# Two grouped attentions: outputs turned by VectorE in blocks of 32 instead of by TensorE, half-groups of 128 tokens by four heads

## The chip, the cores and the metric

The kernel runs on one core of one Trainium2 chip. The time is the device time of one execution in microseconds (us). Three executions of the kernel before took 3545.53, 3547.29 and 3551.32 us; the median, 3547.29 us, is the number to beat. Engines are named as in the profile: PE is TensorE's matmul, PEld its weight load, DVE is VectorE, ACT is ScalarE, POOL is GpSimd, SP is the engine that issues most transfers.

## The reference

Eight layers run one after another on x, 4 batches of 256 tokens by 256 numbers, with a context of 1601 tokens. The change touches the second and the sixth, which are grouped attentions with 16 query heads, 4 key heads and heads of 128 numbers. The sixth, cut to what matters:

```
q = rms_norm((x @ Wq).reshape(B, 256, 16, 128), q_norm_w)
k = rms_norm((ctx @ Wk).reshape(B, S_enc, 4, 128), k_norm_w)
v = (ctx @ Wv).reshape(B, S_enc, 4, 128)
scores = einsum('bhqd,bhkd->bhqk', q, repeat(k, 4)) / 128 ** 0.5
out = einsum('bhqk,bkhd->bqhd', softmax(scores), repeat(v, 4))
x = x + out.reshape(B, 256, 2048) @ Wo
```

The second layer does the same, but its keys and values come from the context and the 256 tokens of x together, and queries and keys are rotated by their positions (`rope`).

## The kernel before

`grouped_attention` is called once for each of the two layers (stage a1 with `rope` True, stage a3 with False). Work is cut into 16 groups, one for each batch and key head. A group holds 4 query heads by 256 tokens, which are 8 blocks of 128 columns, and is done in two units of 512 columns. A unit walks over all key tiles of 128 tokens, 15 in a1 and 13 in a3, and one such tile is a turn.

In each turn PE computes scores for a key tile (`scores`, three products of 512 columns, L1176 to L1178), then does what tasks stand in that turn's entry of `GROUP_TURNS`, then adds probabilities times values of the tile 21 turns back in a1, 19 in a3 (`values`, L1188). ACT moves scores from PSUM into a ring (`keep`, L1309) and takes the exponential of an older tile (`exp`, L1324). DVE keeps the running maximum (`highest`, L1572), subtracts a maximum from some tiles (`shift`, L1589) and POOL subtracts it from the others (`shift`, L1436). Each engine has its own instruction list in a fixed order, and semaphores tie them: `scores` of a turn waits for `highest` of two turns before, because there are two score banks.

In the entries of `GROUP_TURNS`, KV, Q, KX, QX, OX, Y and others are tasks of the next group or the last one. Most use one of three PSUM banks in turn. The tasks that the change touches are these:

- `outputs` on DVE runs when the last value product of a unit is done, in turns 6 and 21 of a group in a1 and in turns 6 and 19 in a3. It divides by the row sums (L1597, L1598) and writes `o_rows`, tokens down and head dimension across. PE's next unit of value products waits for it (`o_done`).
- OX turns `o_rows` for the output product: four PE transposes (L1122) into a bank, ACT's copy into the high half `ot[0]` (L1296), and DVE's subtraction into the low half `ot[1]` (L1489, in the helper `low`). It is in turns 12 and 23 of a1, 8 and 21 of a3.
- Y is the output product, 12 matmuls of 256 columns for each block of 128 tokens (L1133). It waits for OX of both halves.
- QX turns queries for the next group; in the kernel before one half is two heads by 256 tokens.
- `end_turn`, `end_high`, `end_low` and `end_products` do the same for the last group, behind the last turns.

## Time and profile before

| | |
|---|---|
| median of 3 runs | 3547.29 us |
| profiled execution, whole | 3551.81 us |
| profiled execution, span from the first to the last instruction | 3550.1 us |
| first scores of a1 to its last | about 527 to 1621 us of the span |
| first scores of a3 to its last | about 2421 to 3386 us of the span |
| PE busy | 3300.8 us, 93% |
| DVE busy | 2283.9 us, 64% |
| ACT busy | 2250.7 us, 63% |
| POOL busy | 1545.9 us, 44% |

The profile lists single instructions with start, duration, what they write and read, and the idle time of their engine before them with what ended it. Matmuls overlap one another, so what one of them costs is read from the start of the first to the start of what follows, not from its own duration. One value product shows as two matmul records, since the trace has two passes for it, so `values` of a turn are 8 records; a transpose shows as one.

### The profile page before, as it was taken

Reading aid. Unit: us, or ns where it says so; the run is one execution under the profiler, and the core shown is the slowest. Engines: PE = TensorE matmul, PEld = TensorE weight load, DVE = VectorE, ACT = ScalarE, POOL = GpSimd, SP = SyncE. Lnnn points to the kernel's source line nnn. Section 1 sums busy time; section 2 is a strip of 40 time slices with the busy share of each in tenths; the row PEclk is TensorE's granted clock in tenths of the full one; section 3 lists DMA queues with packets and bytes.
Section 4 is the critical chain, followed back from the end, with each engine's and each line's share of the span. In section 5 each row is a group of like instructions: output and inputs, shape, how many; then the busy total and the mean of one; then the engine's idle time right before and its main releaser. Section 6 shows DMA issues by size and latency. Waiting matters only on the chain. (4 is left out here: it accounts for less than half of the span.)

```text
span 3550.1 us, 64164 instructions
## 1 busy us (share of the span) xinstructions
PE 3300.8 (93%) x23332; PEld 2862.7 (81%) x23332; DVE 2283.9 (64%) x4549; ACT 2250.7 (63%) x5204; POOL 1545.9 (44%) x1568
## 2 busy tenths in 40 slices
PE   6858968999999999998899999897999999999999
PEld 5658967999989989997666665586999989999888
DVE  8976756776676676666777777435555555555544
ACT  3326746777777777774566676416777777777743
POOL 0012137767676667663121120203555555555534
PEclk8879979999999999999899999899999999999999
DMA  5206522211120120102101100213211121110011
GB/s 192 93 24 230 210 107 70 86 62 37 43 79 31 37 91 31 37 25 80 44 1 38 38 1 1 77 39 131 76 67 60 43 74 43 69 59 31 30 40 39
DMA packets 74457, 227.83 MB, mean 64 GB/s; under 512 B 7780, under 2 KB 29472, under 8 KB 69152
## 3 DMA queue, kind: packets, MB, share of 16 engines
q1 hardware_dynamic: 67538, 184.04, 14.6%
q0 software_dynamic: 3696, 37.68, 2.8%
q8 instruction: 188, 3.08, 0.4%
q10 hardware_dynamic: 2910, 2.01, 0.2%
q14 instruction: 125, 1.02, 0.1%
HBM read 178.60 MB, written 45.11 MB: 63 GB/s over the span
## 5 line engine op out<-in xcount | busy, mean ns | idle before, releaser
L1188 PE MATMUL ps<-a_v_rows,a_ring 128*128 128x129 f32 (+1 forms) x7168 | 937.2, 276 | 8.0 <-DVE a_o_rows L1598 6.4
L1572 DVE SCALAR_TENSOR_TENSOR a_peak<-ps,a_k_rstd,a_peak 128x512 f32<-128x512 f32 (+1 forms) x768 | 575.9, 750 | 569.5 <-ACT a_ring L1309 559.8
L1309 ACT ACTIVATE a_ring<-ps,a_k_rstd 128x512 f32<-128x512 f32 (+1 forms) x896 | 616.6, 689 | 476.2 <-PE ps L1178 433.3
L1188 PEld LDWEIGHTS ps<-a_v_rows,a_ring 128*128 128x128 f32 (+1 forms) x7168 | 877.5, 192 | 23.6 <-ACT a_ring L1324 7.1
L1436 POOL TENSOR_TENSOR a_ring<-a_ring,a_negb 128x512 f32<-128x512 f32 (+1 forms) x506 | 642.4, 1292 | 236.3 <-ACT a_negb L1318 228.4
L1324 ACT ACTIVATE a_ring<-a_ring 128x512 f32<-128x512 f32 (+1 forms) x896 | 563.6, 632 | 14.5 <-DVE a_ring L1589 9.4
L1176 PE MATMUL ps<-a_qt,a_kt 128*128 128x512 f32 (+1 forms) x896 | 424.6, 474 | 18.6 <-DVE a_peak L1572 14.3
L1076 PEld LDWEIGHTS ps<-a_wr,a_ct 128*128 128x128 f32 (+1 forms) x2496 | 353.0, 189 | 48.1 <-issue 13.6
L1076 PE MATMUL ps<-a_wr,a_ct 128*128 128x256 f32 (+1 forms) x2496 | 373.6, 287 | 13.5 <-DMA a_ct<-ctx_lo 13.3
L1178 PE MATMUL ps<-a_qt,a_kt 128*128 128x512 f32 (+1 forms) x896 | 355.4, 397 | 0.0
L1177 PE MATMUL ps<-a_qt,a_kt 128*128 128x512 f32 (+1 forms) x896 | 354.2, 395 | 0.0
L3431 ACT ACTIVATE a_probs<-ps 128x1024 f32<-128x1024 f32 x224 | 229.6, 1025 | 134.8 <-PE ps L3285 134.0
L1589 DVE TENSOR_TENSOR a_ring<-a_ring,ps 128x512 f32<-128x512 f32 x390 | 263.0, 677 | 2.8 <-ACT a_negb L1318 2.8
L3623 DVE TENSOR_REDUCE a_parts<-ps 128x1 f32<-128x448 f32 x384 | 222.2, 619 | 57.8 <-PE ps L3247 52.4
L1178 PEld LDWEIGHTS ps<-a_qt,a_kt 128*128 128x128 f32 (+1 forms) x896 | 166.1, 185 | 42.6
L1176 PEld LDWEIGHTS ps<-a_qt,a_kt 128*128 128x128 f32 (+1 forms) x896 | 169.3, 189 | 28.7 <-DVE a_peak L1572 20.8
L1177 PEld LDWEIGHTS ps<-a_qt,a_kt 128*128 128x128 f32 (+1 forms) x896 | 169.4, 189 | 1.6
L3285 PE MATMUL ps<-a_qt,a_kt 128*128 128x512 f32 x448 | 163.8, 447 | 2.5 <-ACT a_qt L3418 2.3
L1371 POOL TENSOR_SCALAR a_k_sq<-a_k_sq 128x4 f32<-128x4 f32 (+2 forms) x128 | 29.0, 226 | 311.0 <-ACT a_v_rows L1272 306.6
L1520 DVE TENSOR_TENSOR a_k_rows<-ps,a_kw 128x128 f32<-128x128 f32 (+1 forms) x448 | 126.6, 283 | 56.6 <-ACT a_v_rows L1272 56.4
L3247 PE MATMUL ps<-a_kt,a_qt 128*128 128x448 f32 (+1 forms) x512 | 154.9, 370 | 4.7 <-ACT a_kt L3399 1.1
L1268 ACT ACTIVATE a_square<-ps 128x128 f32<-128x128 f32 (+1 forms) x448 | 124.7, 278 | 33.0 <-PE ps L1076 26.4
(469 smaller groups left out, 6012.9 us busy)
## 6 DMA issues: line engine op xcount, KB each, us to landing
a_wr<-a_w SPq DMA_DIRECT2D x96, 512.0 KB, 4.3
a_w<-a_wr SPq DMA_DIRECT2D x32, 512.0 KB, 3.9
a_wr<-a_w SPq DMA_DIRECT2D x48, 256.0 KB, 3.7
a_ct<-ctx_hi SPq DMA_DIRECT2D x8, 1090.0 KB, 5.8
a_ct<-ctx_lo SPq DMA_DIRECT2D x8, 1090.0 KB, 8.8
f_we<-in_f_experts SPq DMA_DIRECT2D x8, 1088.0 KB, 9.1
ctx_hi<-a_ct SPq DMA_DIRECT2D x4, 1602.0 KB, 5.4
ctx_lo<-a_ct SPq DMA_DIRECT2D x4, 1602.0 KB, 9.4
```

The lines of the kernel that those rows point to most:

```text
L1076: ins = pe.matmul(out[0:r, 0:2 * HD], src, wr[0][v][:, c * 2 * HD:(c + 1) * 2 * HD], start=(n == 0), stop=(n == 3 * DC - 1))
L1176: pe.matmul(out, kt[0][:, at:at + r], qt[0][:, cols], start=True, stop=False)
L1177: pe.matmul(out, kt[0][:, at:at + r], qt[1][:, cols], start=False, stop=False)
L1178: pe.matmul(out, kt[1][:, at:at + r], qt[0][:, cols], start=False, stop=True).then_inc(st_ready, 1)
L1188: ins = pe.matmul(m.ps[:, 6 + i // 2, (i % 2) * 256:(i % 2) * 256 + VW], slot(n)[0:r, i * P:(i + 1) * P], v_rows[u // NG % 2][0:r, t, :], ...
L1309: act.activation(slot(n)[0:r, :], m.ps[0:r, SCORE_BANKS[n % 2], :], ACT.Copy, scale=k_rstd[0:r, g % 2, t:t + 1]).then_inc(kept, 1)
L1324: act.activation(slot(n)[0:r, :], slot(n)[0:r, :], ACT.Exp).then_inc(exp_done, 1)
L1436: pool.tensor_tensor(slot(n)[0:r, :], slot(n)[0:r, :], negb[0:r, u % 2, :], ALU.add)\
L1572: dve.scalar_tensor_tensor(out=peak[0:r, :], in0=m.ps[0:r, SCORE_BANKS[n % 2], :], scalar=k_rstd[0:r, u // NG % 2, t:t + 1], in1=(slot(n - ...
L1589: dve.tensor_tensor(slot(n)[0:r, :], slot(n)[0:r, :], m.ps[0:r, MAX_BANK, :], ALU.add)\
L3431: act.activation(flat2(probs[n % 3][:, :, :]), flat2(m.ps[:, first:first + 2, :]), ACT.Exp)\
L3623: dve.tensor_reduce(to, slot(("R", h, j))[:, 0:n], AX.X, ALU.max, negate=True).then_inc(neg_done, 1)
```

## The change

Three things change together.

First, a unit holds four heads of 128 tokens instead of two heads of 256 tokens. QX transposes the same eight blocks, but ACT and DVE write them so that a block of 128 columns is 4 heads by 32 tokens. Such a block becomes the rows of the unit's output.

Second, OX no longer exists on PE. `outputs` ends with one DVE instruction that transposes every 32 by 32 square of the half of `o_rows` in place. After it, rows are 4 heads by 32 dimensions and columns are tokens, which is a valid left operand of the output product, once the rows of `wo` are laid out in the same order (in `lay_gqa`, before the launch). ACT and DVE then make the high and low halves from `o_rows` in SBUF instead of from a PSUM bank, in the same places of their lists.

Third, Y of a block of 128 tokens needs only its own unit, so it waits for one low half (`o_lo`) and not for both.

```
@@ scores, queries, outputs: views @@
+            def queries_of(k, i):
+                return qt[i][:, k * 512:(k + 1) * 512].rearrange("p (i h t) -> p h i t", h=REP, t=32)
+            def turned_outputs(k, i):
+                return ot[i][:, k * 512:(k + 1) * 512].rearrange("p (b i t) -> p i b t", b=P // 32, t=32)
+            def output_blocks(k):
+                return o_rows[:, k * JG:(k + 1) * JG, :].rearrange("p i (b t) -> p i b t", t=32)
@@ PE @@
                     def QX(g, k):
-                        for i in range(4):
-                            j = 4 * k + i
-                            ins = pe.transpose(out[:, i * P:(i + 1) * P], q_rows[:, j % QT, j // QT, :], m.ident[:, :])
-                    def OX(g, k):
-                        out = begin(("OX", g, k))
-                        pe.wait_ge(o_done, NG * (g - 1) + k + 1)
-                        for i in range(4):
-                            ins = pe.transpose(out[:, i * P:(i + 1) * P], o_rows[:, 4 * k + i, :], m.ident[:, :])
-                        ins.then_inc(item_ready, 1)
+                        for h in range(REP):
+                            ins = pe.transpose(out[:, h * P:(h + 1) * P], q_rows[:, k, h, :], m.ident[:, :])
                     def Y(g, q):
-                        pe.wait_ge(item_free, number[("OX", g, 1)] + 1)
+                        pe.wait_ge(o_lo, NG * (g - 1) + q + 1)
+                        output_products(out, q).then_inc(item_ready, 1)
-                    def end_turn(k):
...
@@ ACT @@
                     def OX(g, k):
-                        act.activation(ot[0][:, k * 512:(k + 1) * 512], begin(("OX", g, k)), ACT.Copy)\
-                           .then_inc(item_act, 1)
+                        act.wait_ge(o_turned, NG * (g - 1) + k + 1)
+                        if ("Y", g - 1, k) in number:
+                            act.wait_ge(item_ready, number[("Y", g - 1, k)] + 1)
+                        act.activation(turned_outputs(k, 0), output_blocks(k), ACT.Copy).then_inc(o_hi, 1)
@@ DVE @@
                     def OX(g, k):
-                        low(("OX", g, k), ot[1][:, k * 512:(k + 1) * 512], ot[0][:, k * 512:(k + 1) * 512], 512)
+                        dve.wait_ge(o_hi, NG * (g - 1) + k + 1)
+                        dve.tensor_tensor(turned_outputs(k, 1), output_blocks(k), turned_outputs(k, 0).bitcast(F32),
+                                          ALU.subtract).then_inc(o_lo, 1)
                     def outputs(u):
                         dve.wait_ge(pv_done, KT * (u + 1))
+                        if u >= NG:
+                            dve.wait_ge(o_hi, u - NG + 1)
...
                            .then_inc(o_done, 1)
+                        dve.wait_ge(o_done, u + 1)
+                        half_rows = flat2(o_rows[:, G * JG:(G + 1) * JG, :])
+                        dve.transpose(half_rows, half_rows).then_inc(o_turned, 1)
@@ end @@
                         if attend and n == END_TURN:
-                            end_turn(0)
...
-                            end_high(0)
+                            OX(GROUPS, 0)
@@ lay_gqa @@
-        f"{name}_wo": np.asarray(wo).reshape(KVH, REP, P, D).transpose(0, 2, 1, 3).reshape(KVH, P, -1),
+        f"{name}_wo": np.asarray(wo).reshape(KVH, REP, P // 32, 32, D).transpose(0, 1, 3, 2, 4).reshape(KVH, P, -1),
```

How the lists change is shown at two places of stage a1, in the sixth group. The first is PE's list at the turn with the second OX (turn 23), between the value products of the turn before and those of the turn after; `a_qt,a_kt` are the scores, `a_wr,a_ct` key and value products of the next group, `a_o_rows` is OX. Before:

```order
L1188 MATMUL ps<-a_v_rows,a_ring 128x129 x8
L1176 MATMUL ps<-a_qt,a_kt 128x512
L1177 MATMUL ps<-a_qt,a_kt 128x512
L1178 MATMUL ps<-a_qt,a_kt 128x512
L1122 MATMUL ps<-ident,a_o_rows 128x128 x4
L1188 MATMUL ps<-a_v_rows,a_ring 128x129 x4
```

After:

```order
L1199 MATMUL ps<-a_v_rows,a_ring 128x129 x8
L1187 MATMUL ps<-a_qt,a_kt 128x512
L1188 MATMUL ps<-a_qt,a_kt 128x512
L1189 MATMUL ps<-a_qt,a_kt 128x512
L1199 MATMUL ps<-a_v_rows,a_ring 128x129 x4
```

The four transposes are gone and nothing else on PE has moved.

The second place is DVE's list from `outputs` in turn 21 to OX in turn 23; `a_peak` is `highest`, `a_ring` is `shift`, `a_k_rows` empties a bank of key and value products. Before:

```order
L1597 RECIPROCAL a_rsum<-ps 128x4 [waits a1_pv_done]
L1598 TENSOR_TENSOR a_o_rows<-ps,a_rsum 128x512 [waits a1_dstep]
L1572 SCALAR_TENSOR_TENSOR a_peak<-ps,a_k_rstd,a_peak 128x512 [waits a1_peaked,a1_kept]
L1589 TENSOR_TENSOR a_ring<-a_ring,ps 128x512 [waits a1_kept,a1_negb_ok]
L1520 TENSOR_TENSOR a_k_rows<-ps,a_kw 128x128 [waits a1_item_act]
L1572 SCALAR_TENSOR_TENSOR a_peak<-ps,a_k_rstd,a_peak 128x512 [waits a1_peaked,a1_kept]
L1520 TENSOR_TENSOR a_k_rows<-ps,a_kw 128x128 [waits a1_item_act]
L1572 SCALAR_TENSOR_TENSOR a_peak<-ps,a_k_rstd,a_peak 128x512 [waits a1_peaked,a1_kept]
L1589 TENSOR_TENSOR a_ring<-a_ring,ps 128x512 [waits a1_kept,a1_negb_ok]
L1489 TENSOR_TENSOR a_ot<-ps,a_ot 128x512 [waits a1_item_act]
```

After:

```order
L1591 RECIPROCAL a_rsum<-ps 128x4 [waits a1_o_hi,a1_pv_done]
L1592 TENSOR_TENSOR a_o_rows<-ps,a_rsum 128x512 [waits a1_dstep]
L1597 STREAM_TRANSPOSE a_o_rows<-a_o_rows 128x512 [waits a1_o_done]
L1564 SCALAR_TENSOR_TENSOR a_peak<-ps,a_k_rstd,a_peak 128x512 [waits a1_peaked,a1_kept]
L1581 TENSOR_TENSOR a_ring<-a_ring,ps 128x512 [waits a1_kept,a1_negb_ok]
L1508 TENSOR_TENSOR a_k_rows<-ps,a_kw 128x128 [waits a1_item_act]
L1564 SCALAR_TENSOR_TENSOR a_peak<-ps,a_k_rstd,a_peak 128x512 [waits a1_peaked,a1_kept]
L1508 TENSOR_TENSOR a_k_rows<-ps,a_kw 128x128 [waits a1_item_act]
L1564 SCALAR_TENSOR_TENSOR a_peak<-ps,a_k_rstd,a_peak 128x512 [waits a1_peaked,a1_kept]
L1581 TENSOR_TENSOR a_ring<-a_ring,ps 128x512 [waits a1_kept,a1_negb_ok]
L1547 TENSOR_TENSOR a_ot<-a_o_rows,a_ot 128x4x4x32 [waits a1_o_hi]
```

One instruction is new, ahead of `highest`, and the subtraction of OX stands where it stood but reads two operands from SBUF where one came from PSUM. ACT's list keeps its order; its copy of OX reads `a_o_rows` and waits for the DVE transpose.

## Rows read from the trace of the kernel before

**Rows 1.** The page's first part: busy us (share of span) xinstructions
```profile
PE 3300.8 (93%) x23332; PEld 2862.7 (81%) x23332; DVE 2283.9 (64%) x4549; ACT 2250.7 (63%) x5204; POOL 1545.9 (44%) x1568
```
**Rows 2.** Stretches of a1 and a3: us, busy of each engine, PEclk, DMA share, GB/s
```profile
860.00:960.00 100.00, 100.00 (x729) 92.35 (x728) 64.63 (x117) 73.15 (x188) 65.24 (x69) 1.00 0.10 33
...
2720.00:2830.00 110.00, 108.94 (x788) 99.63 (x787) 60.57 (x113) 79.98 (x211) 62.77 (x62) 1.00 0.17 59
```
**Rows 3.** PE's waits, first a1, then a3: us in total, times, longest
```profile
PE ps L1176 <- DVE a_peak L1572: 10.5, 9, 3.6
...
PE ps L1155 <- DVE a_ring L1589: 9.1, 17, 0.6
...
PE ps L1133 <- DVE a_ot L1489: 0.2, 1, 0.2
```
**Rows 4.** OX's instructions, by tile: duration ns min/median/max, first and last start, forms
```profile
L1122 PE MATMUL ps<-ident,a_o_rows x240: 270/272/273, 627.9 to 3387.5; 128*128 128x128 f32 x120
...
L1200 PE MATMUL ps<-ident,a_o_rows x16: 272/273/330, 1647.5 to 3422.2; 128*128 128x128 f32 x16
...
L1296 ACT ACTIVATE a_ot<-ps x60: 582/589/591, 628.8 to 3388.0; 128x512 fp32r<-128x512 f32 x60
...
L1489 DVE TENSOR_TENSOR a_ot<-ps,a_ot x60: 678/681/685, 630.1 to 3388.8; 128x512 fp32r<-128x512 f32 x60
```
**Rows 5.** Timeline, a1, turns 23 to 26: start us, us, engine line op [idle before]
```profile
932.95 0.48 PE L1176 MATMUL ps<-a_qt,a_kt 128*128 128x512 f32 x1
...
933.73 0.60 PE L1122 MATMUL ps<-ident,a_o_rows 128*128 128x128 f32 x4
...
934.17 1.06 PE L1188 MATMUL ps<-a_v_rows,a_ring 128*128 128x129 f32 x8
...
934.65 0.75 DVE L1572 SCALAR_TENSOR_TENSOR a_peak<-ps,a_k_rstd,a_peak 128x512 f32<-128x512 f32 x1 [2.01 <-ACT a_ring L1309]
934.98 0.48 PE L1176 MATMUL ps<-a_qt,a_kt 128*128 128x512 f32 x1
...
935.91 0.68 DVE L1489 TENSOR_TENSOR a_ot<-ps,a_ot 128x512 fp32r<-128x512 f32 x1
...
936.69 0.75 DVE L1572 SCALAR_TENSOR_TENSOR a_peak<-ps,a_k_rstd,a_peak 128x512 f32<-128x512 f32 x1
...
939.30 0.47 PE L1176 MATMUL ps<-a_qt,a_kt 128*128 128x512 f32 x1
```
**Rows 6.** Timeline, a1, highest behind outputs in turn 6, scores of turn 8
```profile
896.86 0.74 DVE L1572 SCALAR_TENSOR_TENSOR a_peak<-ps,a_k_rstd,a_peak 128x512 f32<-128x512 f32 x1
...
899.12 0.47 PE L1176 MATMUL ps<-a_qt,a_kt 128*128 128x512 f32 x1
```
**Rows 7.** Timeline, highest behind outputs: a1 turn 21, a3 turn 6 with scores
```profile
930.04 0.75 DVE L1572 SCALAR_TENSOR_TENSOR a_peak<-ps,a_k_rstd,a_peak 128x512 f32<-128x512 f32 x1
...
2555.30 0.75 DVE L1572 SCALAR_TENSOR_TENSOR a_peak<-ps,a_k_rstd,a_peak 128x512 f32<-128x512 f32 x1
...
2558.16 0.48 PE L1176 MATMUL ps<-a_qt,a_kt 128*128 128x512 f32 x1
```
**Rows 8.** DVE lines with two SBUF operands: duration ns min/median/max
```profile
L3645 DVE TENSOR_TENSOR a_o_rows<-a_o_n x16: 291/292/1402, 1773.8 to 2259.7; 128x128 f32<-128x128 f32 x16
...
L1476 DVE TENSOR_TENSOR a_wr<-a_wf,a_wr x16: 681/1226/1994, 565.3 to 2665.4; 128x1024 fp32r<-128x1024 f32 x12, 128x512 fp32r<-128x512 f32 x4
```
**Rows 9.** POOL's shift, the page's fifth part: busy us, mean ns of one
```profile
L1436 POOL TENSOR_TENSOR a_ring<-a_ring,a_negb 128x512 f32<-128x512 f32 (+1 forms) x506 | 642.4, 1292 | 236.3 <-ACT a_negb L1318 228.4
```
**Rows 10.** Timeline, the end of a1
```profile
1648.13 0.60 ACT L1335 ACTIVATE a_ot<-ps 128x512 fp32r<-128x512 f32 x1 [3.17 <-PE ps L1200]
...
1649.30 7.41 PE L1188 MATMUL ps<-a_v_rows,a_ring 128*128 128x129 f32 x64 [0.31 <-ACT a_ring L1324]
...
1660.17 0.69 DVE L1598 TENSOR_TENSOR a_o_rows<-ps,a_rsum 128x512 f32<-128x512 f32 x1
...
1661.62 0.60 ACT L1335 ACTIVATE a_ot<-ps 128x512 fp32r<-128x512 f32 x1 [7.70 <-PE ps L1200]
```

More of the change, by code:

```diff
@@ L862, in grouped_attention @@
         shifted_dve = st.sem("shifted_dve")
+        o_turned, o_hi, o_lo = [st.sem(n) for n in "o_turned o_hi o_lo".split()]
         pre = (pre0, pre1, pre2)
-        end_turned, end_hi, end_lo, end_ready, end_done = [
-            st.sem(n) for n in "end_turned end_hi end_lo end_ready end_done".split()]
+        end_ready, end_done = st.sem("end_ready"), st.sem("end_done")
         def peaks(n):
@@ L886, in run @@
             flat = [task for turn in turns for task in turn]
-            items = [t for t in flat if t[0] in ("PX", "NX", "KV", "Q", "KX", "QX", "OX", "Y", "MX")]
+            items = [t for t in flat if t[0] in ("PX", "NX", "KV", "Q", "KX", "QX", "Y", "MX")]
             number = {task: i for i, task in enumerate(items)}
@@ L1127, in Y, with output_products @@
                         wait_weights(pe, g, 2)
-                        pe.wait_ge(item_free, number[("OX", g, 1)] + 1)
+                        pe.wait_ge(o_lo, NG * (g - 1) + q + 1)
+                        output_products(out, q).then_inc(item_ready, 1)
+                    def output_products(out, q):
                         n = 0
-                        for h in range(REP):
-                            j = h * QT + q
+                        for b in range(P // 32):
+                            j = q * (P // 32) + b
                             for s, v in HALVES:
                                 ins = pe.matmul(out[:, 0:D], ot[s][:, j * P:(j + 1) * P],
-                                                wr[2][v][:, h * D:(h + 1) * D],
-                                                start=(n == 0), stop=(n == 3 * REP - 1))
+                                                wr[2][v][:, b * D:(b + 1) * D],
+                                                start=(n == 0), stop=(n == 3 * (P // 32) - 1))
                                 n += 1
-                        ins.then_inc(item_ready, 1)
+                        return ins
                     def MX(g, i):
@@ L1192, in values, with end_products @@
                         ins.then_inc(pv_done, 1)
-                    def end_turn(k):
-                        if k == 0:
-                            pe.wait_ge(item_free, len(items))
-                        pe.wait_ge(o_done, UNITS - NG + k + 1)
-                        for i in range(JG):
-                            ins = pe.transpose(m.ps[:, 2 + k, i * P:(i + 1) * P], o_rows[:, k * JG + i, :], m.ident[:, :])
-                        ins.then_inc(end_turned, 1)
-                    def end_products(k):
-                        if k == 0:
+                    def end_products(q):
+                        if q == 0:
                             pe.wait_ge(kept, TURNS)
@@ L1208, in end_products @@
                             wait_weights(pe, GROUPS, 2)
-                        pe.wait_ge(end_lo, k + 1)
-                        for q in range(QT):
-                            for n, (h, s, v) in enumerate((h, s, v) for h in range(k * REP // NG, (k + 1) * REP // NG)
-                                                          for s, v in HALVES):
-                                j = h * QT + q
-                                ins = pe.matmul(m.ps[:, q, 0:D], ot[s][:, j * P:(j + 1) * P],
-                                                wr[2][v][:, h * D:(h + 1) * D], start=(k == 0 and n == 0),
-                                                stop=(k == NG - 1 and n == 3 * REP // NG - 1))
-                            if k == NG - 1:
-                                ins.then_inc(end_ready, 1)
-                    does = {"PX": PX, "NX": NX, "KV": KV, "Q": Q, "KX": KX, "QX": QX, "OX": OX, "Y": Y, "MX": MX, "NB": NB}
+                        pe.wait_ge(o_lo, UNITS - NG + q + 1)
+                        output_products(m.ps[:, q, :], q).then_inc(end_ready, 1)
+                    does = {"PX": PX, "NX": NX, "KV": KV, "Q": Q, "KX": KX, "QX": QX, "Y": Y, "MX": MX, "NB": NB}
                     for n, turn in enumerate(turns):
@@ L1232, in _ @@
                                 values(v)
-                        if attend and n == END_TURN:
-                            end_turn(0)
                         if attend and n == END_LOW:
```

33 lines of the change are left out of this document (14 added, 19 removed).

## The prediction

> **What bounds the kernel now.** I read the page's first part, then stretches of the two stages that the change touches, then PE's waits in them, then the instructions of the task OX, and last the timeline around that task and around `outputs`.
>
> PE is busy for 93% of the whole span, the other engines for at most 64% [rows 1]. In the stretches it is clearer: in the middle of a1 PE has work in all of 100 us, in a3 in 108.94 of 110, at a granted clock of 1.00, while DVE is busy for 65 and 61 us and ACT for 73 and 80 [rows 2]. The reader should see that no other engine comes near, and that POOL, at 65 and 63, doesn't either. Busy PE is not yet PE as the bound, so the waits decide: in the whole of a1 PE waited for the running maximum 9 times, 10.5 us in sum, and the most frequent wait of a3 is 9.1 us in 17 times, for a subtraction on DVE before the maximum is spread [rows 3]. That is 1% of each stage. So inside a1 and a3 an instruction taken from PE is time taken from the kernel, and an instruction given to DVE costs nothing until it makes PE wait.
>
> **What is removed from PE.** OX is 240 transposes, four at a time, so 60 tasks; 16 more transposes stand in the ends of the two stages [rows 4]. Each shows 272 ns, but they overlap. The cost of a task is from its first start to the start of the next line: 933.73 to 934.17, 0.44 us [rows 5]. I take 0.435, since the times are rounded, and 60 x 0.435 = 26.1 us. Of the four tasks at the ends, the first of each stage stands among value products that PE does back to back, which is 2 x 0.435 = 0.9 us. The second of each is in a chain of single steps and comes below. No weight load and no column is added: Y keeps its 12 matmuls of 256 columns, QX its four transposes, scores their 512 columns. The weights' new order is made before the launch.
>
> **What ACT and DVE do instead.** ACT's copy took 589 ns and DVE's subtraction 681 ns with a PSUM operand [rows 4]; both remain in their places, with `o_rows` in SBUF as source and in pieces of 32 columns. By the nearest rows of 512 columns I leave both at their durations, bounded by 0.3 us (a two-operand DVE instruction on SBUF with 128 columns) and 1.23 us (one with 1024) [rows 8].
>
> The new instruction is the DVE transpose, 64 times, 128x512. No transpose on DVE is in this trace. The nearest row is the product just before it, 128x512 in 0.69 us [rows 10]; from below it is bounded by the 0.29 us of 128 columns and from above by the 1.23 us of 1024 columns [rows 8]. I take 0.69.
>
> What hides it: it stands ahead of `highest`, for which PE waits only two turns later. In turn 6 of a1 `highest` ends at 896.86 + 0.74 = 897.60 and the scores that need it start at 899.12, so 1.52 us are free [rows 6]. For turn 21 it is 930.79 against 932.95, 2.16 us [rows 5, 7], and in a3 2556.05 against 2558.16, 2.11 us [rows 7]. So 0.69 is hidden at each, and so is 1.23. PE's new unit of value products waits for the product before the transpose and not for the transpose. Queued behind it on DVE are `highest`, a shift and the emptying of a bank; the idle 2.01 us of DVE ahead of turn 23's `highest` [rows 5] take up the delay before OX comes. ACT's wait for the transpose is no wait, since OX is two turns or more later.
>
> The exception is the second group of a1, where DVE still gathers the results of the layer before. PE already waits for `highest` in these first groups [rows 3]. There I charge one transpose in full, +0.7 us.
>
> By the Trainium skill (VectorE: DVE Perf Modes, "The three transpose paths") a VectorE transpose of 128x128 in bf16 takes 311 ns, works in blocks of 32x32 and stands beside 390 ns for TensorE. Four of these would be an estimate of 1.24 us from that page, for a narrower type than ours. The sum would then change by some 0.5 us in the second group of a1 and at each end; no run here shows a DVE transpose, so the trace can't say yet.
>
> **The turn without OX.** In turn 23 PE needs 934.98 - 932.95 = 2.03 us [rows 5] and would need 1.59. DVE has 0.75 + 0.68 + 0.68 = 2.11 in it, with the shift taken like the subtraction [rows 5]. It falls 0.5 us behind, which the next turns can absorb if the margin holds: `highest` behind OX ends at 936.69 + 0.75 = 937.44 and is needed at 939.30, so 1.86 us are free, 1.42 after PE gets 0.44 faster [rows 5]. So the full 0.435 is kept.
>
> DVE's subtraction now reads both operands from SBUF, and such instructions sometimes wait in this trace: a 128x128 one takes 291 ns, but in its slowest instance 1402 [rows 8]. The added 1.11 us is about what POOL may have left of one 1.29 us shift [rows 9]. The one before, with a PSUM operand, never took over 685 ns in 60 times [rows 4]. So up to 1.29 us can come on top, and 1.42 us are free. I charge nothing.
>
> The Trainium skill (GPSIMD Engine Reference, "Specifications") says that GpSimd shares its SBUF interfaces with VectorE, with contention for DVE instructions that have two SBUF inputs. By that rule the trace agrees, and the change moves 64 instructions to the contended kind; by the rule alone each could lose a POOL instruction's length, which is the second rival below.
>
> **The ends.** At the end of a1 ACT sat idle for 3.17 us until PE had turned the first half, with exponentials queued behind the copy, and PE then waited 0.31 us for an exponential [rows 10]. ACT no longer waits for PE there; -0.3 us for each stage, -0.6. In the last step, from the end of the product (1660.86) to ACT's copy (1661.62) it was 0.76 us over PE [rows 10]; 0.69 and two handoffs of about 0.04 over DVE are as long. The last 12 matmuls are as many as before. Y's looser wait is worth nothing: PE waited there once in a3, 0.2 us [rows 3].
>
> Sum: -26.1 - 0.9 - 0.6 + 0.7 = -26.9 us. The profiled execution took 3551.81 us with a span of 3550.1, so it would take 3524.9. It lay 4.5 us over the median of the runs, 3547.29, so the median becomes 3520.4.
>
> **The rivals.**
>
> *A, the turn doesn't shrink in a1.* Without OX, DVE's 2.11 us stand against PE's 1.59. If the backlog is not absorbed, the 30 turns of a1 stay at about 2.03 and only a3's 30 give their 0.435: -13 us, 3534. For it speaks that DVE has no idle time between OX and the next `highest`; against it the 1.86 us of margin [rows 5]. 10%.
>
> *B, collisions with POOL come onto the path.* POOL is busy for 0.65 of the time [rows 2] and has half of a 1.29 us instruction left on average, 0.65 us. Fully exposed that is 60 x 0.65 x 0.65 = 25 us and eats the gain: between 3534 for half of it and 3546 for all. It also holds POOL back. Against it stand the margins of 1.42 us and more; it needs back-to-back POOL work in which DVE loses more than one instruction, and the 1994 ns of a 1024-column row [rows 8] is the longest of that line. 6%, most of it near 3534.
>
> *C, slower: the DVE transpose of 4-byte numbers is several passes.* With a duration T, the margins give 15 x (T - 1.52) + 15 x (T - 2.16) + 30 x (T - 2.11) = 60T - 118.5 of waiting for `highest` when T is above all of them. From T = 2.41 us on this exceeds the 26 us that are saved. Four passes of 0.69 are 2.76 us and make +47 - 27 = +20: 3567. Nothing in the profile speaks for it but that no DVE transpose is there; against it, every 512-column DVE row is near 0.7 us. 4%.
>
> **How the numbers follow.** The forecast has 80% and its own range is 3516 to 3526: down if the small PE waits of a1 shrink too and by the spread of the runs, up by some exposed delays. A has 10%, B 6%, C 4%. The range of 8 in 10 reaches from 3514 to 3532 and leaves out C, most of B and the longer half of A. A difference under 0.2%, 7 us, can't be told from none. Faster by more: the forecast, A, and half of B, 93%. Within: 3%. Slower: 4%.
>
> **What would show it.** Right: no PE transposes of `a_o_rows`; turn 23 of a1 at 1.6 us between two scores; 64 DVE transposes of 0.6 to 0.8 us; PE's waits for `a_peak` still near 10 us in a1. Some subtractions of OX stretched to 1 to 2 us without a PE wait two turns later. Wrong: scores two turns behind `outputs` that wait for `a_peak` (C), scores two turns behind OX that do (A, B), or exponentials that come late behind a held POOL. The prediction fails if the transpose takes over 1.5 us or if PE idles over 20 us more in the two stages.

## The result and the profile after

The changed kernel took 3532.46 us, the median of five runs (3520.77 to 3535.25), beside 3550.23 for the kernel before. The ratio is 0.9945, with an interval of 0.9934 to 0.9956. Run twice more in other groups of runs it gave 0.9945 and 0.9943. By the medians that is 17.8, 18.7 and 20.4 us less; by the ratios it is 19.5 to 20.2, and the interval of the first reaches from 15.6 to 23.4. The forecast had 26.9 us and 3520.4; applied to the 3547.29 of the start, the ratio gives 3527.8, and the median of its own runs lies half a microsecond above the range's end of 3532. The direction was right; a quarter of the gain didn't come.

First a correction of the table ahead of the prediction: it has the bounds of the two stages some 10 us too early. From first to last scores, a1 of the kernel before ran from 537.5 to 1631.7 and a3 from 2432.0 to 3396.5. No term of the sum rests on it.

The page's first part and two stretches of the kernel after, which answer to [rows 1, 2]:

```profile
PE 3264.8 (93%) x23076; PEld 2831.8 (80%) x23076; DVE 2333.8 (66%) x4613; ACT 2247.6 (64%) x5204; POOL 1561.2 (44%) x1568
```
```profile
1100.00:1200.00 100.00, 100.00 (x733) 92.92 (x733) 66.43 (x121) 76.11 (x198) 77.20 (x79) 1.00 0.11 38
2900.00:3010.00 110.00, 109.47 (x797) 100.98 (x796) 65.27 (x117) 80.63 (x212) 60.96 (x60) 1.00 0.10 37
```

PE has 256 instructions fewer and DVE 64 more. PE is as full as before; POOL's busy time grew by 15 us though it has the same 1568 instructions.

The instructions that took the place of those in [rows 4], as durations in ns (min/median/max):

```profile
L1597 DVE STREAM_TRANSPOSE a_o_rows<-a_o_rows x64: 711/711/716, 610.2 to 3388.8; 128x512 f32<-128x512 f32 x64
L1289 ACT ACTIVATE a_ot<-a_o_rows x64: 614/621/630, 622.9 to 3389.5; 128x512 fp32r<-128x512 f32 x64
L1547 DVE TENSOR_TENSOR a_ot<-a_o_rows,a_ot x64: 673/683/1792, 624.3 to 3390.2; 128x512 fp32r<-128x512 f32 x64
```

The DVE transpose takes 0.71 us each time, where 0.69 was taken. The subtraction keeps its median of 0.68 us, but 16 of the 64, one in each group of a3, are stretched, most of them to 1.79.

Turn 23 of the same group of a1 as in [rows 5], in the timeline after:

```profile
925.83 0.48 PE L1187 MATMUL ps<-a_qt,a_kt 128*128 128x512 f32 x1
...
926.61 1.05 PE L1199 MATMUL ps<-a_v_rows,a_ring 128*128 128x129 f32 x8
...
927.41 0.48 PE L1187 MATMUL ps<-a_qt,a_kt 128*128 128x512 f32 x1
...
927.52 0.75 DVE L1564 SCALAR_TENSOR_TENSOR a_peak<-ps,a_k_rstd,a_peak 128x512 f32<-128x512 f32 x1 [1.50 <-ACT a_ring L1301]
...
928.79 0.68 DVE L1547 TENSOR_TENSOR a_ot<-a_o_rows,a_ot 128x512 fp32r<-128x512 f32 x1
...
929.39 0.74 DVE L1564 SCALAR_TENSOR_TENSOR a_peak<-ps,a_k_rstd,a_peak 128x512 f32<-128x512 f32 x1
```

From scores to scores it is 927.41 - 925.83 = 1.58 us, where the forecast had 1.59. `highest` behind OX ends at 930.13 and the scores that need it start at 931.75, a margin of 1.62.

Now the waits of PE, as total, times and longest, in a1 and then in a3, as in [rows 3]:

```profile
PE ps L1187 <- DVE a_peak L1564: 13.6, 14, 3.6
```
```profile
PE ps L1166 <- DVE a_ring L1581: 9.1, 17, 0.6
```

In a3 nothing has changed. In a1 PE waits five more times for the running maximum, 3.1 us more.

To find the rest I divided each execution at the first and the last scores of a1 and of a3. The times are us; in brackets stand the us that the trace's clock record has at half clock in that part:

```
               up to a1      a1             between       a3            behind a3
before         537.5 (159)   1094.1 (15.4)  800.3 (84)    964.5 (5.1)   153.6 (13.7)
after          532.8 (151)   1084.4 (9.4)   797.2 (80)    950.2 (5.2)   154.5 (17.1)
difference      -4.8           -9.7          -3.1         -14.4          +0.9
```

a3 gave 14.4, more than its 30 x 0.435 = 13.1. a1 gave only 9.7. Of these 9.7 us, 2.9 lie in turn 22 of group 0 and turn 7 of group 3, which ran at half clock in the profile of before and not in this one. A later execution of the changed kernel, with 15.7 us of a1 at half clock beside the 15.4 of before, gained 6.8 us in a1. The sum is 31 us, because this profiled execution was the quickest one of the changed kernel; its part up to a1 and the one behind a3 are not typical, as the experiments show. Two profiled executions alone would have put the gain half as large again as it is.

Groups and turns are counted from 0 here, and a turn is measured from the start of its scores to the start of the next. Turn by turn, the OX turns of a1 and a3 are 0.43 to 0.46 us shorter, each of them. Against that, turns 0 and 1 of groups 3, 7 and 11, in which work for the next batch begins, are 1.08 to 1.11 and 0.44 us longer. I call these places the batch changes. Here is DVE ahead of group 7, before and after:

```profile
1017.71 1.68 DVE L1645 TENSOR_SCALAR a_ang_tmp<-a_ang_tmp 128x960 f32<-128x960 f32 x1
1019.31 0.73 DVE L1572 SCALAR_TENSOR_TENSOR a_peak<-ps,a_k_rstd,a_peak 128x512 f32<-128x512 f32 x1
```
```profile
1009.54 3.50 DVE L1642 TENSOR_SCALAR a_ang_tmp<-a_ang_tmp 128x960 f32<-128x960 f32 x1
1012.96 0.74 DVE L1564 SCALAR_TENSOR_TENSOR a_peak<-ps,a_k_rstd,a_peak 128x512 f32<-128x512 f32 x1
```

It is the last of the steps that make the angles for the next batch (task RA8), which the diff doesn't touch. It took 1.67 to 1.69 us and takes 3.48 to 3.50. POOL meanwhile, in the kernel after:

```profile
1009.28 1.31 POOL L1424 TENSOR_TENSOR a_ring<-a_ring,a_negb 65x512 f32<-65x512 f32 x1
1010.54 1.02 POOL L1379 TENSOR_TENSOR a_by_sin<-a_k_rows,a_cs 128x384 f32<-128x384 f32 x1
1011.52 1.00 POOL L1380 TENSOR_TENSOR a_by_cos<-a_k_rows,a_cs 128x384 f32<-128x384 f32 x1
1012.60 1.56 POOL L1424 TENSOR_TENSOR a_ring<-a_ring,a_negb 128x512 f32<-128x512 f32 x1
```

Three POOL instructions without a gap, and the DVE step ends 0.52 us after the third of them. In the kernel before, POOL's instructions also stood without a gap, but the step ended 0.51 us after the one that was under way when it started, and POOL's next one took 1.42 us instead of 1.02:

```profile
1017.46 1.42 POOL L1436 TENSOR_TENSOR a_ring<-a_ring,a_negb 65x512 f32<-65x512 f32 x1
1018.84 1.42 POOL L1391 TENSOR_TENSOR a_by_sin<-a_k_rows,a_cs 128x384 f32<-128x384 f32 x1
```

Why one POOL instruction goes ahead of the step there and three here is not shown. Then PE, after the change:

```profile
1013.75 0.50 PE L1187 MATMUL ps<-a_qt,a_kt 128*128 128x512 f32 x1 [0.83 <-DVE a_peak L1564]
...
1014.95 0.66 PE L1155 MATMUL ps<-ident,a_peak 128*128 128x128 f32 x4 [0.23 <-DVE a_qt L1542]
```

This is the mechanism of rival B, at an instruction that I had not priced, with a single SBUF operand.

The end of a3 after the change, which answers to the last rows of [rows 10] in its structure:

```profile
3385.87 1.95 PE L1199 MATMUL ps<-a_v_rows,a_ring 128*128 128x129 f32 x16
3390.95 1.83 PE L1144 MATMUL ps<-a_wr,a_ot 128*128 128x256 f32 x12 [3.13 <-DVE a_ot L1547]
3396.02 3.63 PE L2223 MATMUL ps<-ident,f_z 128*128 128x128 f32 x16 [3.23 <-DVE f_z L2352]
3401.69 3.89 PE L2239 MATMUL ps<-f_zt,f_wr 128*128 128x512 f32 x10 [2.04 <-DVE f_zt L2358]
```

PE sits idle for 3.13 us in one piece. Before, four transposes stood in the middle of that time:

```profile
3418.84 1.95 PE L1188 MATMUL ps<-a_v_rows,a_ring 128*128 128x129 f32 x16
3421.79 0.66 PE L1200 MATMUL ps<-ident,a_o_rows 128*128 128x128 f32 x4 [1.00 <-DVE a_o_rows L1598]
3423.86 2.93 PE L1214 MATMUL ps<-a_wr,a_ot 128*128 128x256 f32 x12 [1.41 <-DVE a_ot L1649]
```

### The profile page after: what moved, and what is told of

Same layout as the page of the kernel before. It is cut to its first block and busy times, and to the rows that moved or that the text cites. A ratio compares the mean times of both kernels' runs of the same rounds, so it can differ in the third digit from the quotient of the medians.

```text
span 3519.0 us, 63774 instructions
## 1 busy us (share of the span) xinstructions
PE 3264.8 (93%) x23076; PEld 2831.8 (80%) x23076; DVE 2333.8 (66%) x4613; ACT 2247.6 (64%) x5204; POOL 1561.2 (44%) x1568
## 5 line engine op out<-in xcount | busy, mean ns | idle before, releaser
L1424 POOL TENSOR_TENSOR a_ring<-a_ring,a_negb 128x512 f32<-128x512 f32 (+1 forms) x506 | 649.9, 1306 | 236.9 <-ACT a_negb L1310 229.0
L1092 PE MATMUL ps<-a_wr,a_ct 128*128 128x256 f32 (+1 forms) x2496 | 371.2, 286 | 13.9 <-DMA a_ct<-ctx_lo 13.7
L3242 PE MATMUL ps<-a_kt,a_qt 128*128 128x448 f32 (+1 forms) x512 | 153.8, 367 | 4.7 <-ACT a_kt L3394 1.1
```

Source lines behind the costliest of these rows:

```text
L1092: ins = pe.matmul(out[0:r, 0:2 * HD], src, wr[0][v][:, c * 2 * HD:(c + 1) * 2 * HD], start=(n == 0), stop=(n == 3 * DC - 1))
L1424: pool.tensor_tensor(slot(n)[0:r, :], slot(n)[0:r, :], negb[0:r, u % 2, :], ALU.add)\
```

## The experiments

All ratios are to the kernel before, run on the same chip in the same group of runs.

**The changed kernel, run again**, to see how far a profile repeats. No edit.

> The changed kernel once more, without an edit. Its profiled execution had a span 31.1 us shorter than the profiled one of before, but the median of its runs is only 17.8 us shorter, and its runs reach from 3520.8 to 3535.3 us at mean granted clocks of 0.963 down to 0.957. Theory 1: the runs differ in where PE's clock is low, and the typical run has some 10 us more of low clock in stretches in which PE is the bound. Then a profile at 3530 us or more shows a half-clock stretch within the two grouped attentions or a longer one ahead of them. Theory 2: the runs differ in the collisions of DVE with POOL; then such a profile has the same clock rows and longer DVE instructions. If the profile comes out near 3520 us again, neither is told apart, and the runs alone give the spread.

3531.82 us, ratio 0.9945 (0.9931 to 0.9958). a1 was 1084.6 us and a3 950.2 us long, within 0.2 of the first. Up to a1 it took 538.9 us and behind a3 156.7, 6.1 and 2.2 us more. Inside the attentions these two executions agree to 0.2 us, and their difference lies outside. That isn't always so: in the third execution, below, a1 took 2.9 us more, all of it in two stretches at half clock. The pair speaks for theory 1: up to a1 this execution was at half clock for 164.5 us instead of 151, and behind a3 for 24 instead of 17, while every turn of a1 and a3 is within 0.1 us of the first execution's.

**PE's time put back.** Four transposes of the identity into the score bank, ahead of the scores of each OX turn; DVE keeps its part.

```diff
+if ("OX", g, 0) in turns[n] or ("OX", g, 1) in turns[n]:
+    for i in range(4):
+        pe.transpose(m.ps[:, SCORE_BANKS[n % 2], i * P:(i + 1) * P], m.ident[:, :], m.ident[:, :])
```

> The changed kernel with PE's cost put back: four transposes of the identity into the score bank ahead of the scores of each turn that has OX, 240 in all; nothing reads them. If PE's time is what the change gains (my forecast), this costs 60 x 0.435 = 26 us over the changed kernel and lies within 5 us of the kernel before. If the gain came from the freed PSUM bank, from the looser wait of the output products or from the halves being done apart, it stays within 7 us of the changed kernel.

3546.86 us, ratio 0.9989 (0.9980 to 0.9998). The 0.44 us came back once for each OX task, ahead of its scores; a1 grew by 12.7 us and a3 by 13.1, so 25.8 of the 26.1 that 60 x 0.435 make. (In a1 two stretches at half clock took 3.1 us more, and shorter turns elsewhere gave about as much back.) So the gain inside the stages goes when PE's time comes back, though all that the change does on the other engines stays. The median rose by 15 us only, and is 3.6 us below that of the kernel before; in its profile the part behind a3 was 151.5 us long, the shortest so far, which opened the question of what happens there. RA8 took 3.48 to 3.50 us here too, so it isn't the shorter PE time alone that brings it against POOL.

**The DVE transposes left out.** The outputs then aren't transposed; the semaphore is raised by an empty instruction.

```diff
-dve.transpose(half_rows, half_rows).then_inc(o_turned, 1)
+dve.engine_nop().then_inc(o_turned, 1)
```

> The changed kernel without the DVE transposes (64 left out; rows and output product are then taken in the wrong order, so the output is not the reference's). If one transpose is hidden, as forecast, the two stages keep their length: within 2 us in a3, and in a1 only the group starts that came out longer (+1.5 us in turns 0 and 1 at each change of batch) may move. If the transposes cost something in each group, a1 and a3 get shorter by 0.1 us or more per group.

3524.84 us, ratio 0.9927 (0.9911 to 0.9942). The steady groups of a1 (68.14 us) and of a3 (61.1) are the same to 0.02 us as with the transposes: they are hidden, as forecast. a1 as a whole was 1.7 us longer; two places at half clock make +3.1 of it, turn 0 of groups 7 and 11 got 0.4 shorter each (that of group 3 did not), and turn 25 of group 2 got 0.5 shorter. So the transposes cost about 1.4 us in a1 in all. RA8 stays at 3.49. The median is 7 us lower all the same (3523.4 to 3526.2 beside 3527.4 to 3533.5), more than the stages show. At its ends PE's wait is 2.44 us instead of 3.13, and the part behind a3 took 153.7 us with 13.7 at half clock, 3 us less than the changed kernel run beside it: a second sign of the ends. The rest of the 7 us isn't located, so the transposes aren't shown to be free for the kernel as a whole.

**Five DVE transposes in place of one**, chained.

```diff
+for _ in range(4):
+    step(dve.transpose(half_rows, half_rows))
 dve.transpose(half_rows, half_rows).then_inc(o_turned, 1)
```

> The changed kernel with five DVE transposes in a row in place of one, each waiting for the one before (five give what one gives). One takes 0.711 us in the profile, so with about 0.05 us of waiting between them T is 3.8 us. By the margins read from the trace of before, 60T - 118.5 = 109 us more PE waiting than with a transpose below 1.5 us: about 3640. If transposes were already on the path, the slope would be 60 x 3.1 = 185 us, 3715. If DVE's idle time between the turns could take up more than the first score wait shows, it is under 60 us.

3656.91 us, ratio 1.0304 (1.0289 to 1.0320), so 125 us over the changed kernel where 109 was expected. a1 grew by 72.6 us and a3 by 51.3. PE's waits in a3, in one row:

```profile
PE ps L1187 <- DVE a_peak L1564: 41.5, 33, 2.2
```

So scores two turns behind `outputs` wait for `highest`, by the formula of rival C. In a steady group of a3 the two turns grew by 1.56 and 1.51 us. The first transpose starts at 613.3 and the last at 616.2, so five take 616.2 + 0.71 - 613.3 = 3.6 us, and 3.6 - 2.11 = 1.5. The formula of rival C gives 98 us for a T of 3.6. What the stages have beyond that goes at least in part with the clock: 36.7 us of a1 were at half clock instead of 9.4, and 12.0 of a3 instead of 5.2.

**One PE transpose of four in the kernel before.** Three quarters of the turned outputs aren't made.

```diff
-                        for i in range(4):
+                        for i in range(1):
                             ins = pe.transpose(out[:, i * P:(i + 1) * P], o_rows[:, 4 * k + i, :], m.ident[:, :])
```

> The kernel before, with one of the four PE transposes in each OX task (the other three are left out, so three quarters of the turned outputs are not made). Nothing moves to DVE, and the copies keep their PSUM operand. Theory 1, the gain is the PE time of the transposes: each OX turn gets about 3/4 of 0.435 = 0.33 us shorter, 60 x 0.33 = 19.6 us in a1 and a3 together. Theory 2, the gain came with the chain behind them (no bank, no PSUM operand, no rotation of banks): clearly less than 10 us. On the step RA8 at a batch change: if the shift of PE's turns brings it against POOL, it takes 3.5 us here too; if the SBUF operands of the copies do, it stays at 1.7.

3544.06 us, ratio 0.9971 (0.9959 to 0.9983): 10 us gained, not 19.6. Every OX turn got 0.33 us shorter, in a1 and in a3, as Theory 1 has it. But in a3 the turn behind the second OX grew by 0.32 in each group. There Y needs the subtraction of the turn just before, and PE now arrives early; the matmuls of Y begin 0.51 us behind the start of the last score instruction, where they would follow in 0.23:

```profile
2959.82 0.40 PE L1178 MATMUL ps<-a_qt,a_kt 128*128 128x512 f32 x1
2960.33 1.66 PE L1133 MATMUL ps<-a_wr,a_ot 128*128 128x256 f32 x12
```

```profile
2959.50 0.68 DVE L1489 TENSOR_TENSOR a_ot<-ps,a_ot 128x512 fp32r<-128x512 f32 x1
```

In the changed kernel the same subtraction is no earlier against PE, and yet Y doesn't wait, because its wait is for the other half, done 14 turns before:

```profile
2939.86 0.40 PE L1189 MATMUL ps<-a_qt,a_kt 128*128 128x512 f32 x1
2940.10 1.57 PE L1144 MATMUL ps<-a_wr,a_ot 128*128 128x256 f32 x12
```

```profile
2939.66 0.68 DVE L1547 TENSOR_TENSOR a_ot<-a_o_rows,a_ot 128x512 fp32r<-128x512 f32 x1
```

Y starts at 2940.10 and the subtraction ends at 2940.34. With the wait of before, and the 0.15 us that lie there between that end and Y's start, Y would have come 0.39 us later; that is an estimate of 6 us over 15 groups.

In a1 a gain of 9.9 us shrank to 4.1 by RA8 (3 x 1.07), by turns 7 and 8 of group 11 (1.6, with 3.4 us at half clock there) and by turn 17 of three groups (0.9). So neither theory had it whole. PE's time is the gain, but in a3 nearly half of it is kept only because the third part of the change also loosens Y's wait. I had called that worth nothing. RA8 took 3.49 us here as well, with neither a DVE transpose nor an SBUF operand added. Several different small shifts bring it there.

**RA8 moved**, to turn 1 of the next group, or to turn 27 ahead of the token normalisation.

```diff
-"MX1 KR7<",
+"MX1 KR7< RA8<",
-"KV14 RA8 GP14",
+"KV14 GP14",
```

> The changed kernel, with the last step of the angles (RA8: 128x960, one SBUF operand, DVE) moved from turn 29 of the group before to turn 1 of the group that begins a batch. Theory P, a block: in the changed kernel this step takes 3.5 us instead of 1.7 because three POOL instructions stand back to back while it wants SBUF, and PE's first scores of groups 3, 7 and 11 then wait 0.83 us for the running maximum and 0.23 us for the queries. Moved, turns 0 and 1 of these groups get 1.0 to 1.5 us shorter together, a1 gets 3 to 4.5 us shorter than in the changed kernel, unless the step meets as full a POOL in turn 1 (then the same is lost two turns later). Theory Q, the first turns of a batch are long for another reason (the new queries and the change of the key buffers): the 3.5 us move with the step, and turns 0 and 1 stay as they are. a3 unchanged by both; time by P about 3527, by Q 3531.

```diff
-"KV13 KR5 NZ0 GP13", "KV14 RA8 GP14",
+"KV13 KR5 RA8 NZ0 GP13", "KV14 GP14",
```

> The changed kernel, with the same step moved two turns earlier, to turn 27, ahead of the token normalisation NZ. Theory P: as with the other move, -3 to -4.5 us in a1, if POOL has a gap there; if it meets back-to-back POOL instructions there too, it takes 2.5 to 3.5 us again and the loss moves to turns 28 and 29, and a1 stays. Theory Q: turns 0 and 1 of groups 3, 7 and 11 stay as long as in the changed kernel wherever the step stands.

3527.73 us (ratio 0.9930, 0.9916 to 0.9943) and 3529.61 us (the same ratio and interval), with 3552.97 for the kernel before. In both the turns 0 and 1 of groups 3, 7 and 11 are 1.1 and 0.44 us shorter, so 4.6 us in a1. Theory P holds and Q falls. In turn 27 the step takes 0.65 us:

```profile
1014.68 0.65 DVE L1642 TENSOR_SCALAR a_ang_tmp<-a_ang_tmp 128x960 f32<-128x960 f32 x1
```
```profile
1014.43 1.82 POOL L1386 TENSOR_TENSOR a_k_rows<-a_by_cos,a_by_sin 128x256 f32<-128x256 f32 x1
1016.22 0.78 POOL L1387 TENSOR_TENSOR a_k_rows<-a_by_cos,a_by_sin 128x256 f32<-128x256 f32 x1
```

Here DVE isn't held, and the POOL instruction beside it and the DVE step that follows takes 1.82 us, where its median in this run is 0.735. In turn 1 the step took 1.50. The total of a1 fell by 1.9 and 2.7 us only, since turn 22 of group 0 (in both) and turn 7 of group 7 (in the first) were 1.5 us longer, with 6.3 and 2.7 us more of a1 at half clock. The two ratios' intervals overlap that of the unmoved kernel, so by the medians of these runs alone the gain isn't told from none; the pair with both edits, below, tells it.

**The kernel before, once more**, with a profile.

> The kernel before, once more, for a second profile of it. If the spread of the runs lies outside the two attention stages, a1 is 1094.1 and a3 964.5 us long again, within 0.5 us but for a stretch at half clock, while the time up to a1 and behind a3 differs from 537.5 and 153.6 by up to 6 us in sum. If the spread lies inside them, they differ by several us.

a1 1094.2 us, a3 963.8, behind a3 153.8. Up to a1 534.1 instead of 537.5, between the attentions 804.6 instead of 800.3. So the part behind a3 was 153.6 and 153.8 in the two profiles of before, while in those of the changed kernel with and without RA8 moved it was 154.5, 156.7, 156.5 and 156.6. That difference of about 3 us is the second term of the shortfall. a1 agreed to 0.1 us and a3 to 0.8.

**PE kept busy at the ends.** 24 transposes of the identity into a bank that nobody reads, in the wait of 3.13 us; alone, and with RA8 in turn 27 as well.

```diff
+if q == 1:
+    pe.wait_ge(item_free, len(items))
+    for i in range(24):
+        pe.transpose(m.ps[:, 2, i % 4 * P:(i % 4 + 1) * P], m.ident[:, :], m.ident[:, :])
 pe.wait_ge(o_lo, UNITS - NG + q + 1)
```

> The changed kernel, with 24 transposes of the identity (128x128, into a bank that nobody reads) on PE at the end of each attention stage, in the 3.1 us in which PE waits for the last halves of the outputs; at 0.11 us each they take 2.6 us and lie in the wait. In the profiles so far the part behind a3 has 17 to 24 us at half clock and takes 154.5 to 156.7 us with the change, 13.7 us and 153.6 to 153.8 us before. Theory C: the clock falls there because PE idles for 3.13 us in one piece, where before it had transposes in between; filled, the part has 14 us or less at half clock and takes 154 us or less, up to 3 us shorter. Theory F, it is the chance of where the falls lie: it has 17 to 24 us again and takes 154.5 to 157 us. By both the stages a1 and a3 keep their 1084.5 and 950.2 us.

> The changed kernel with the angles' last step in turn 27 and the 24 transposes at the end of each attention stage. By theory P for the first and theory C for the second it takes 2.7 us and up to 3 us less than the changed kernel, about 3525 to 3527; by theory F for the second the same as with the moved step alone, about 3528. a1 1081.7 to 1082.6 us, a3 950.2 us.

> The changed kernel a third time, on the same chip as the two above. a1 and a3 are 1084.5 and 950.2 us long again, within 0.3 us but for a stretch at half clock, which costs 1.5 us; behind a3 17 to 24 us at half clock if theory C holds, 10 to 24 if F does. Median 3530 to 3533.

The three ran on one chip. The changed kernel took 3530.84 us (3530.4 to 3533.2), with the ends filled 3525.92 (3524.0 to 3527.5), with both edits 3520.81 (3519.9 to 3525.3); the kernel before 3551.21. The ratios are 0.9943 (0.9931 to 0.9954), 0.9926 (0.9914 to 0.9938) and 0.9915 (0.9901 to 0.9928). The part behind a3, less its last 3 us, in the windows of before, of the changed kernel, of the filled one and of the one with PE's time put back (length, busy us of PE, PEld, DVE, ACT and POOL, then the granted clock):

```profile
3396.50:3547.10 150.60, 140.50 (x846) 124.38 (x844) 70.84 (x186) 54.22 (x91) 61.32 (x44) 0.95 0.13 42
```
```profile
3372.10:3525.70 153.60, 141.45 (x837) 125.25 (x836) 71.98 (x188) 54.02 (x91) 61.17 (x44) 0.92 0.14 41
```
```profile
3373.50:3522.10 148.60, 140.24 (x862) 124.95 (x860) 71.90 (x188) 54.02 (x91) 61.19 (x44) 0.97 0.14 43
```
```profile
3391.50:3540.00 148.50, 137.79 (x838) 122.42 (x836) 71.93 (x188) 54.08 (x91) 61.24 (x44) 0.97 0.13 43
```

The first three clock rows read 0.95, 0.92 and 0.97, which are 13.7, 23.9 and 10.2 us at the lower of the two levels, 1.2 GHz. The fourth has 10.2 us too. The filled end in the timeline:

```profile
3396.61 2.79 PE L1214 MATMUL ps<-ident 128*128 128x128 f32 x24
3399.91 1.68 PE L1144 MATMUL ps<-a_wr,a_ot 128*128 128x256 f32 x12 [0.51 <-DVE a_ot L1551]
```

a1 and a3 were 1087.5 and 950.5 us long in it, and 1087.4 and 950.4 in the changed kernel beside it. So a1 was 3 us longer in both than the 1084.5 that I had expected: turn 22 of group 0 and turn 7 of group 7 each took 1.5 to 1.6 us more, with a fall of the clock in each. The part behind a3 was 5.0 us shorter with the filling, where I had expected up to 3; in the version with both edits it was as short. The part between the attentions was 3.4 us shorter in this pair, but two executions without the filling have the same 797 us there. Up to a1, where nothing differs, it took 4.7 longer. So what the filling is shown to give lies behind a3, and theory F falls. What the trace shows is the order of events: PE idle for 3.13 us, the granted clock at its lower level within 2 us (from 3392.3 on in the first profile, where the idle piece ended at 3390.95), and PE's work in the part behind then longer. This order stands in five of the six profiles that have the 3.13 us. The sixth is the one with PE's time put back: there PE is idle for 3.13 us and then for 3.24, as in the others, the clock falls only behind the second piece, and the whole has 10.2 us at half clock, as if the wait were filled. So theory C is right about what the filling does, and the idle piece alone doesn't decide whether the clock falls.

The version with both edits is the quickest of all, 30 us under the kernel before. It is 5.1 us quicker than the one with the filling alone, and a1 is 4.1 us shorter in it: that is what the moved step gives. Together that is 10 us, where I had expected under 6.

**The same filling in the kernel before**, in its two waits of 1.00 and 1.41 us: is this a loss of the change, or had the kernel before it too?

```diff
+if k == 1:
+    for i in range(8):      # 11 ahead of the products
+        pe.transpose(m.ps[:, 4, i % 4 * P:(i % 4 + 1) * P], m.ident[:, :], m.ident[:, :])
```

> The kernel before, with 8 and 11 transposes of the identity on PE in its two waits at the end of each attention stage (1.00 us for the last rows of the outputs, 1.41 us for the last subtraction). In the changed kernel the wait is one piece of 3.13 us, and filling it brought 5 us. Theory C1, the single long piece is what the change lost there: the kernel before has 13.7 us at half clock behind a3 and little to win, so the filling brings 0 to 2 us. Theory C2, any idle time there costs as much, and the change lost nothing by it: the filling brings 4 to 5 us here too.

3550.38 us, ratio 1.0005 (0.9995 to 1.0014). Nothing is gained, so C2 falls. Without the filling the first fall behind a3 comes 27.1 us behind the last scores and takes 3.4 us, and another of 3.4 us comes at 33.9; with it there is one of 6.8 us at 33.9. Both have 13.7 us at half clock. That fits C1, by which the one long piece, new with the change, is what costs; the profile with PE's time put back, which has that piece at no cost, stands against C1 as a rule.

## Why the prediction was partly right

**The main term, right.** 60 tasks by 0.435 us: each OX turn got shorter by 0.43 to 0.46, and putting the time back took 25.8 us.

**Hidden work, right in the steady groups.** The transpose of 0.71 us costs nothing there. The margins of 1.52, 2.16 and 2.11 us were sound: with five transposes the wait in a3 came out as duration less margin, 1.5 us. The 0.7 us charged to the second group of a1 was in the wrong place: that group is as long with the transposes as without (69.13 and 69.17 us), and they cost 0.5 us in the third group and 0.4 in each of two later ones (groups 2, 7 and 11, counted from 0). The second group did get 0.55 us longer, by 1.38 in turn 17 against the 0.88 of its OX turns, but not by the transpose. The estimate from the Trainium skill (VectorE: DVE Perf Modes, "The three transpose paths"), 1.24 us from four times the bf16 figure, was far from the measured 0.71, though it too would have been hidden.

**Rivals.** A fell: the turn shrank to 1.58 us in a1. C fell by the duration, and its formula held turn by turn in a3, while the total of the test was 125 us against 98 by the formula. B had the right mechanism and the wrong victim. OX's subtraction was stretched in 16 of 64 cases, by up to 1.11 us as the bound from [rows 8] said, and no steady turn paid. The Trainium skill (GPSIMD Engine Reference, "Specifications") names as contended the DVE instructions with two SBUF inputs and also those in a 2-port perf mode; the prediction used only the former. The trace agrees for the first kind, and shows the longest wait of all at an instruction with a single SBUF operand. The Trainium skill (VectorE: DVE Perf Modes, "Two Vector instructions with no wait between them") says that a one-input instruction in a 2-port mode reads through the interface shared with GpSimd. RA8's 0.65 to 3.50 us for the same work fit that, though the trace doesn't show in which mode it ran.

**What failed, first: "So inside a1 and a3 an instruction taken from PE is time taken from the kernel."** It holds for the turn and not for the stage. Shifting PE by 0.43 us also shifts which POOL and DVE instructions meet. RA8 went from 1.7 to 3.5 us at three batch changes, 3 x 1.53 = 4.6 us. I had read POOL's busy share and priced a collision only for the instruction that the diff changes.

**What failed, second: the ends.** "In the last step ... 0.69 and two handoffs of about 0.04 over DVE are as long" is true of the time: PE's last matmuls start 3390.95 - 3385.87 = 5.08 us behind the start of the last value products, and before 3423.86 - 3418.84 = 5.02. But the step was priced by its length alone. It now leaves PE idle in one piece of 3.13 us, and behind a3 the granted clock is lower for about 10 us more: 156.5 to 156.7 us in four of the five profiles of the changed kernel with and without RA8 moved, against 153.6 and 153.8, so 3 us. The Trainium skill (TensorE: Matmul & The Clock Gate, "Part 1: The HAM clock gate") says that the clock follows how busy PE has been of late, and that where it changes varies from run to run. The trace agrees with the second: the first fall of a whole execution of the changed kernel came at 26.2 us once and at 33.6 another time. It agrees with the first in that filling the wait raised the granted clock behind a3 from 0.92 to 0.97, but the run with PE's time put back reads 0.97 with the wait unfilled. So the cost of 3 us is measured, and its cause is shown only in part.

**The sum as it should have been:** -26.9 + 4.6 + 3.0 = -19.3 us. Measured: 0.55% of 3550 us, -19.5. That the two meet so closely is in part chance: the interval is 4 us wide to each side, a3 gave about 1 us more than its term, turns 21, 22 and 25 of group 2 took 1.3 us back, and the part between the attentions varies by 3 us from one execution of the changed kernel to the next.

**A term that was right by luck.** Y's looser wait was put at nothing. The 0.2 us that PE waited there before was read as what the wait could ever cost, but without OX's transposes PE reaches Y 0.44 us sooner. With one transpose of four and the old wait, Y in a3 gives back 0.32 us in each group. In the changed kernel Y starts 0.24 us before the subtraction ends that it used to wait for, so the old wait would have taken some 6 us of the 13 of a3, as estimated above. The main term came out in full only because the change loosens this wait as well; the sum was right, and the reason given for the term was not.

**Left open:** why turn 17 of group 1 of a1 got 1.38 us longer, and that of groups 6 and 10 0.70 shorter, which cancel; why turns 21 and 22 of group 2 got 0.65 longer, with the DVE transposes and without; and what decides the 6 us by which the part up to a1 differs between executions of one kernel. With PE's time put back the same 3.13 us of idle time cost nothing behind a3 (151.5 us). What else decides whether such a piece costs anything isn't known from these runs.

## What to carry to other kernels

When PE is the bound, price the removed PE work by the turn, and then look at the instructions that weren't touched: list the long DVE steps on SBUF with no margin behind them, and see which POOL instructions each would meet when everything ahead moves by half a microsecond. Price a wait of PE by what follows it as well as by its length: a single idle piece where there were two short ones was followed by a lower clock in five profiles of six, and throw-away work put into it gained 5 us. When a wait is loosened along with an edit, test it apart: a wait that costs nothing now can be the next one to bind. Divide a profile at fixed points and take the gain of each part; the total of two profiled executions was 31 us here and the gain by many runs about 19.5.

## What the runs showed of the hardware

- A DVE transpose of 128x512 f32 in blocks of 32 takes 0.711 us, in place and in one instruction, hardly more than a product of the same size (0.691).
- A DVE instruction with one SBUF operand (128x960) takes 0.65 us when it gets ahead of POOL, 1.50 or 1.68 in other places, and 3.50 when it ends behind three POOL instructions that follow each other without a gap. POOL's instructions are longer beside such steps too: one with a median of 0.735 us took 1.82.
- Behind a3, 10 us more at half clock went with about 3 us more of time (13.7 us and 153.6; 23.9 and 156.6).
- Behind the last scores of a3, with PE idle for 3.13 us in one piece, the granted clock was 0.92 over some 153.6 us in four profiles; with the same work and 24 transposes in the wait it was 0.97. In one profile with the same idle piece it was 0.97 as well.
